# Cross attention of a perceiver layer: text probabilities and image sums travel with the image probabilities through DRAM, in halves, and a tile's queries are made between text and image scores

## The reference, cut to what matters

```python
HEADS = 16; DIM_HEAD = 64; INNER = 1024; TEXT_LEN = 77; IMG_SCALE = 1.0
def _attend(q, k, v):
    sim = jnp.einsum('bihd,bjhd->bhij', q, k) * SCALE
    attn = jax.nn.softmax(sim, axis=-1)
    out = jnp.einsum('bhij,bjhd->bihd', attn, v)
...
# Wq, Wk, Wv (text), Wk_ip, Wv_ip (image), Wo, bo
# x + (attend(q, k_text, v_text) + attend(q, k_image, v_image)) Wo + bo
```

## Time and profile before

| | |
|---|---|
| median of 3 runs | 2460.3 us (2457.01 to 2460.98) |
| the profiled execution | 2435.73 us |
| its span | 2433.6 us |
| TensorE matmul busy | 2160.2 us (89%) |
| VectorE busy | 1570.4 us (65%) |
| ScalarE busy | 925.0 us (38%) |
| GpSimd busy | 877.5 us (36%) |
| probabilities stored, loaded | 512 and 512 DMAs of 192 KB |

### The profile page before, as it was taken

One profiled execution on the slowest core, in us unless ns is written; L12 is line 12 of the kernel. 1 busy time (PEld: TensorE's weight loads), 2 busy tenths in 40 slices (PEclk: granted clock), 3 DMA queues, 4 the chain that ended last, 5 costly groups with the idle time before them and its releaser, 6 DMA issues. The chain is left out here.

```text
span 2433.6 us, 37422 instructions
## 1 busy us (share of the span) xinstructions
PE 2160.2 (89%) x13637; PEld 1726.1 (71%) x13637; DVE 1570.4 (65%) x2756; ACT 925.0 (38%) x1869; POOL 877.5 (36%) x535
## 2 busy tenths in 40 slices
PE   5878877796699999999999999999999997787897
PEld 3445545464598889888898998998998994334684
DVE  4179934333577677677677677777776763795554
ACT  1166611210244344344344444444443443452331
POOL 1066412431343333243343333343333300362455
PEclk8989977798899999999999999999999998798898
DMA  5800002511476677677676777776776656001364
GB/s 159 169 16 14 8 1 88 230 50 57 145 200 184 185 218 205 185 217 206 185 217 180 226 202 208 198 207 199 202 211 186 194 156 248 4 0 44 98 148 114
DMA packets 229957, 362.99 MB, mean 149 GB/s; under 512 B 41920, under 2 KB 197824, under 8 KB 225168
## 3 DMA queue, kind: packets, MB, share of 16 engines
q1 hardware_dynamic: 223008, 342.08, 48.1%
q0 software_dynamic: 6768, 18.49, 3.2%
HBM read 234.97 MB, written 125.50 MB: 148 GB/s over the span
## 5 line engine op out<-in xcount | busy, mean ns | idle before, releaser
L2271 PE MATMUL img_ps<-cn,pt_hi 128*128 128x256 f32 (+1 forms) x3072 | 569.7, 287 | 3.0 <-DVE pt_lo L2478 3.0
L2271 PEld LDWEIGHTS img_ps<-cn,pt_hi 128*128 128x128 f32 (+1 forms) x3072 | 477.3, 191 | 3.2 <-issue 3.2
L2271 PE MATMUL img_ps<-cn,pt_lo 128*128 128x256 f32 (+1 forms) x1536 | 435.9, 284 | 0.0
L2466 DVE STREAM_TRANSPOSE prob_blocks<-prob 128x384 f32<-128x384 f32 x512 | 250.6, 547 | 183.8 <-ACT prob L2402 175.9
L2248 PE MATMUL s_ps<-ct,a_hi 128*128 128x508 f32 x768 | 315.7, 411 | 0.0
L2249 PE MATMUL s_ps<-ct,a_hi 128*128 128x508 f32 x768 | 304.2, 396 | 0.0
L2250 PE MATMUL s_ps<-ct,a_lo 128*128 128x508 f32 x768 | 304.0, 396 | 0.0
L2001 POOL TENSOR_SCALAR ct<-staged 128x762 fp32r<-128x762 f32 x64 | 136.8, 2138 | 439.6 <-DMA staged<-in_ctx_t 312.5
L2271 PEld LDWEIGHTS img_ps<-cn,pt_lo 128*128 128x128 f32 (+1 forms) x1536 | 292.6, 190 | 0.0
L2478 DVE TENSOR_TENSOR pt_lo<-prob_moved,pt_hi 128x768 fp32r<-128x768 f32 x256 | 277.9, 1124 | 9.4 <-ACT pt_hi L2414 9.2
L2001 POOL TENSOR_SCALAR cn<-staged 128x768 fp32r<-128x768 f32 x64 | 137.4, 2147 | 376.5 <-DMA staged<-in_ctx_n 293.4
(11 more groups left out here) (370 smaller groups left out, 3712.9 us busy)
## 6 DMA issues: line engine op xcount, KB each, us to landing
prob_rows<-prob_blocks SPq DMA_DIRECT2D x512, 192.0 KB, 2.1
prob_moved<-prob_rows SPq DMA_DIRECT2D x512, 192.0 KB, 3.6
staged<-in_ctx_n SPq DMA_DIRECT2D x64, 384.0 KB, 4.7
staged<-in_ctx_t SPq DMA_DIRECT2D x64, 381.0 KB, 4.7
up_all_m<-in_up SPq DMA_DIRECT2D x8, 2048.0 KB, 12.8
down_all_m<-in_down SPq DMA_DIRECT2D x8, 1024.0 KB, 23.4
sums_m<-y_b SPq DMA_DIRECT2D x63, 128.0 KB, 2.2
w_shared<-in_wq SPq DMA_DIRECT2D x7, 1024.0 KB, 7.3
```

The source lines that it names most:

```text
L2271: last = nc.tensor.matmul(img_ps[:, 0:D], left[0:n, j, :], rows[0:n, right, j, :], start=j == 0 and at == 0, stop=j == IB - 1 and at == 2)
L2466: nc.vector.transpose(blocks[:, m], source[:, m]).then_inc(turned, 1)
```

## The change

The probabilities' DRAM round trip carries a bundle of 15 blocks of 128 columns instead of 12: the 12 image blocks of step g, one block with the scaled text probabilities of step g-3 and two with the scaled image sums of step g-3. So the three TensorE transposes and their copies are gone, and `value_side` reads its operands from `moved`, one iteration later than the transposes of that bundle (LAG = 3, loops to N + LAG + 2). The bundle is turned and stored in two halves instead of four quarters; it is loaded in four parts as before, 240 KB each. The text exponentials get buffers of their own.

`sums` multiplies `pt_hi` with both parts of `cn` in one matmul of 512 columns, into both halves of the bank, and `pt_lo` with the high part into the second half. ScalarE scales the second half into `prob`, VectorE scales the first half and adds it there. At a boundary the queries are made between text and image scores, and their copies come first on ScalarE and VectorE. The projection moves to iteration 4 of a tile, ahead of the sums. The bias is loaded within the stage into `head_out` and added on POOL before batch 1 is split. Text keys are loaded per batch (77 columns), Wq and Wo in two halves.

```diff
@@ load_stage @@
-            sp.dma_start(k.bo1[:], src["bo1"]).then_inc(rest_in, 16)
-            sp.wait_ge(rest_in, 48)
+            sp.wait_ge(rest_in, 32)
@@ cross_attention, sizes and buffers @@
-    RUN = IB * QR
+    TXT_AT, O_AT = IB, IB + 1
+    BUNDLE = IB + 1 + C
+    RUN = BUNDLE * QR
+    LAG = 3
+    PARTS = 2
+    PQ = Q // PARTS
...
-        prob = sb("prob1", [P, TXT + IB * P])
-        blocks = sb("prob_blocks", [P, Q, IB, QR])
-        block_rows = nc.dram_tensor("prob_rows", (2, Q, P, RUN), F32).ap()
-        moved = [sb(f"prob_moved{s}", [P, Q, IB, QR]) for s in range(2)]
+        prob = sb("prob1", [P, BUNDLE * P])
+        txt_prob = [sb(f"txt_prob{s}", [P, TXT]) for s in range(3)]
+        blocks = sb("prob_blocks", [P, Q, BUNDLE, QR])
+        block_rows = nc.dram_tensor("prob_rows", (2, PARTS, P, PQ, RUN), F32).ap()
+        moved = [sb(f"prob_moved{s}", [P, Q, BUNDLE, QR]) for s in range(2)]
         pt_hi, pt_lo = sb("pt_hi", [P, IB, P], F32R), sb("pt_lo", [P, IB, P], F32R)
-        pt_txt = [sb(f"pt_txt{s}", [P, P]) for s in range(3)]
...
+        bo = head_out[:, 0:C, :].rearrange("p c n -> p (c n)")
@@ SP @@
+                cols = slice(b % 2 * TXT, (b % 2 + 1) * TXT)
+                sp.dma_start(k_txt[:, heads], k.k_txt[b // 2][:, heads, cols]).then_inc(k_in, 16)
...
+            sp.dma_start(bo, src["bo1"]).then_inc(bo_in, 16)
...
-            for g in range(N):
+            for g in range(N + LAG):
                 s, (i, b, p, n) = g % 2, parts(g)
                 if g >= 2:
                     sp.wait_ge(moved_in[s], 16 * Q * (g // 2))
+                for u in range(PARTS):
+                    sp.wait_ge(turned, PARTS * g + u + 1)
+                    sp.dma_start(block_rows[s, u].rearrange("p m f -> p (m f)"),
+                                 blocks[:, quarters(u)].rearrange("p m j r -> p (m j r)")).then_inc(stored[u], 16)
+                if g >= 2:
+                    sp.wait_ge(split_done, 2 * min(g - 1, N))
+                if g > LAG + 1:
+                    sp.wait_ge(valued, g - LAG - 1)
                 for m in range(Q):
-                    sp.wait_ge(turned, Q * g + m + 1)
-                    sp.dma_start(block_rows[s, m], blocks[:, m].rearrange("p j r -> p (j r)")).then_inc(stored[m], 16)
-                if g >= 2:
-                    sp.wait_ge(split_done, 2 * (g - 1))
-                for m in range(Q):
-                    sp.wait_ge(stored[m], 16 * (g + 1))
+                    if m % PQ == 0:
+                        sp.wait_ge(stored[m // PQ], 16 * (g + 1))
                     sp.dma_start(moved[s][m * QR:(m + 1) * QR].rearrange("c a j r -> c a (j r)"),
-                                 block_rows[s, m].rearrange("(a c) f -> c a f", a=Q)).then_inc(moved_in[s], 16)
+                                 block_rows[s, m // PQ, :, m % PQ].rearrange("(a c) f -> c a f", a=Q)).then_inc(moved_in[s], 16)
+                if g >= N:
+                    continue
                 if g // PAIRS1 + 1 < NB:
                     load(g // PAIRS1 + 1, g % PAIRS1)
-                if n == 0 and i:
+                if p == 0 and g:
                     sp.wait_ge(scored, g)
-                    load_keys(i, 1)
+                    load_keys(g // PAIRS1, 1)
+                if p == 4 and g // PAIRS1 + 1 < NB:
+                    sp.wait_ge(scored, g)
+                    load_keys(g // PAIRS1 + 1, 0)
+                if n in (5, 6) and 1 <= i < NT - 1:
+                    sp.wait_ge(projected, i)
+                    sp.dma_start(wq[:, n - 5], src["wq1"][:, n - 5]).then_inc(wq_in, 16)
+                if n == 6 and i:
+                    sp.wait_ge(valued, i * STEPS)
+                    load_values(i, 1)
+                if n == 13 and i < NT - 1:
+                    sp.wait_ge(valued, i * STEPS + PAIRS1)
+                    load_values(i + 1, 0)
+                if n < 2 and i:
+                    heads = slice(n * PAIRS1 // 2, (n + 1) * PAIRS1 // 2)
                     sp.wait_ge(queried, i + 1)
-                    sp.dma_start(wo, src["wo1"]).then_inc(wo_in, 16)
-                if n == 4 and i:
-                    sp.wait_ge(v_used, 2 * i)
-                    load_values(i, 1)
-                if n == 5 and 1 <= i < NT - 1:
-                    sp.wait_ge(projected, i)
-                    sp.dma_start(wq, src["wq1"]).then_inc(wq_in, 16)
-                if n == 12 and i < NT - 1:
-                    sp.wait_ge(scored, i * STEPS + 12)
-                    load_keys(i + 1, 0)
-                if n == 13 and i < NT - 1:
-                    sp.wait_ge(v_used, 2 * i + 1)
-                    load_values(i + 1, 0)
+                    sp.dma_start(wo[:, heads], src["wo1"][:, heads]).then_inc(wo_in, 16)
@@ GpSimd @@
             split(0, range(4, 8))
+            pool.wait_ge(bo_in, 16)
+            nc.gpsimd.tensor_tensor(k.x[:], k.x[:], bo.unsqueeze(1).broadcast_to([P, NT, D]),
+                                    ALU.add).then_inc(bo_added, 1)
             split(1)
-            nc.gpsimd.tensor_tensor(k.x[:], k.x[:], k.bo1[:].unsqueeze(1).broadcast_to([P, NT, D]),
-                                    ALU.add).then_inc(bo_added, 1)
@@ TensorE @@
-            def turn_text(g):
-
-                bank = use()
-                pe.wait_ge(txt_normed, g + 1)
-                nc.tensor.transpose(t_ps[bank][0:TXT, 0:P], prob[:, 0:TXT], k.ident).then_inc(t_done[bank], 1)
...
-                        for at, (left, right) in enumerate(((pt_hi, 0), (pt_hi, 1), (pt_lo, 0))):
-                            last = nc.tensor.matmul(img_ps[:, 0:D], left[0:n, j, :], rows[0:n, right, j, :],
-                                                    start=j == 0 and at == 0, stop=j == IB - 1 and at == 2)
+                        nc.tensor.matmul(img_ps[:], pt_hi[0:n, j, :], rows[0:n, :, j, :], start=j == 0, stop=False)
+                        last = nc.tensor.matmul(img_ps[:, D:2 * D], pt_lo[0:n, j, :], rows[0:n, 0, j, :],
+                                                start=False, stop=j == IB - 1)
...
+                back = moved[(g + LAG) % 2]
+                pe.wait_ge(moved_in[(g + LAG) % 2], 16 * Q * ((g + LAG) // 2 + 1))
                 heads = [(t_ps[bank][r * S:(r + 1) * S, 0:S], slice((2 * p + r) * HD1, (2 * p + r + 1) * HD1),
-                          slice(r * S, (r + 1) * S)) for r in range(2)]
+                          slice(2 * r, 2 * r + 2)) for r in range(2)]
                 for c in range(C):
                     for out, cols, rows in heads:
-                        nc.tensor.matmul(out, wv[:, c, cols], ot[:, c, rows], start=c == 0, stop=False)
+                        nc.tensor.matmul(out, wv[:, c, cols], back[:, rows, O_AT + c, :], start=c == 0, stop=False)
                 for out, cols, rows in heads:
-                    last = nc.tensor.matmul(out, v_txt[0:TXT, b, cols], pt_txt[g % 3][0:TXT, rows],
+                    last = nc.tensor.matmul(out, v_txt[0:TXT, b, cols], back[0:TXT, rows, TXT_AT, :],
...
-            for g in range(N + 3):
+            for g in range(N + LAG + 2):
                 if g < N:
                     if g:
                         pe.wait_ge(exp_done, g)
                     kept(a_place)
                     text_scores(g)
+                    if boundary(g):
+                        if g > STEPS:
+                            pe.wait_ge(wq_in, 32 * (g // STEPS) + 16)
+                        q_places = queries(g // STEPS + 1)
                     scores(g)
-                if 1 <= g <= N:
-                    turn_text(g - 1)
-                if g >= 3:
-                    ot_place = turn_sums(g - 3)
-                if boundary(g):
-                    if g > STEPS:
-                        pe.wait_ge(wq_in, 16 * (g // STEPS) + 16)
-                    q_places = queries(g // STEPS + 1)
-                elif g < N - 1:
+                if g < N - 1:
+                    if boundary(g):
+                        for place in q_places:
+                            kept(place)
                     a_place = key_side(g + 1)
+                if projects(g) is not None:
+                    project(projects(g), head_place)
                 if 2 <= g <= N + 1:
                     sums(g - 2)
-                if boundary(g):
-                    for place in q_places:
-                        kept(place)
-                    a_place = key_side(g + 1)
-                if g >= 3:
-                    if g == 3:
+                if LAG + 1 <= g <= N + LAG:
+                    if g == LAG + 1:
                         pe.wait_ge(wv_in, 16)
-                    kept(ot_place)
-                    value_side(g - 3)
-                if projects(g) is not None:
-                    project(projects(g))
+                    value_side(g - LAG - 1)
+                    head_place = ring.place(1)
@@ ScalarE @@
+                if 2 <= g <= N + 1:
+                    act.wait_ge(summed, g - 1)
+                    act.wait_ge(inv_done, g - 1)
```

(29 more changed lines are left out.)

125 lines of the change are left out of this document (44 added, 81 removed).

## The result

The changed kernel took 2498.7 us, median of 4 runs (2491.9 to 2508.6), beside 2460.6 for the kernel before (4 runs, 2457.0 to 2463.5): ratio 1.016, 95% interval 1.013 to 1.019. A second set of runs (E1) gave 1.017 (1.014 to 1.021). The forecast was 2400, range 2374 to 2442.

A forecast was written before the change was run, and what follows sets the result against it. TensorE's own instructions were taken to bound the step. Gains 63 + 20 + 4 + 5 = 92 less 31.5 lost net 60.5 us: 2435.7 profiled becomes 2375, carried over to the runs' median as 2400, range 2374 to 2442.

The forecast's parts named there:

- The return: Bundle's DRAM round trip before the value side: landing S+13.6 to 13.7 (S: start of its first reduction); 15 us lost.
- The loop of two steps: From a bundle's reductions through its value side: with landing L, step is the larger of 9.62 and (L + 5.15)/2.
- the ride: Text probabilities and sums carried in the bundle, replacing three TensorE transposes per step; the transposes' removal was priced at 42 us.
- Tail: Stage's end: last sums pass transposes, store and loads before the value side; 8.5 us plus 1 for lower clock, 9.5 lost.
- The unheld step: Plain cross attention step on TensorE: 0.50 us shorter, 9.62 instead of 10.12; 63 us over 128 steps.
- The transposes: Text transpose and two transposes of the sums removed from TensorE: 0.33 us a step, 42 us over 128 steps.
- Boundaries: Queries of a new tile placed before the image scores, removing waits and low clock: 20 us gained, bounds 13 and 23.
- The bias: Output bias addition on POOL moved from step 8 to the stage's start: 5 us gained, 2 lost at the start.
- the 512 column term: Sums on TensorE in 12 matmuls of 512 and 12 of 256 columns: 0.16 us a step, 21 us saved.
- The term of 5 us for VectorE: VectorE's last operation in contested steps ends at S+9.66 against 9.62, late by under 0.1 us: 5 us lost in all.
- the slower rival: Return landing past S+15.4 makes steps 10.26 and eats all other gains; at S+16, step 10.58 and 2499 us; chance 0.11.
- The sign named beforehand: Forecast wrong if the value side waits in every step; it expected waits for the return in some steps only.

The follow-up runs named there:

- E1: The changed kernel run again without alteration, beside the kernel before on the same chip: 2487.5 us, ratio 1.017.
- E10: Changed kernel, loads leaving out three of the 15 blocks from the third step on, stores unchanged: 2408.7 us, 0.982 of the kernel before.
- E11: Changed kernel with no context loaded from batch 2 on: 2483.7 us, 1.013 of the kernel before.
- E7: Changed kernel with each context piece cut to 48 KB from batch 2 on: 2462.7 us, 1.004 of the kernel before.
- E3: Changed kernel with the bundle turned and stored in four quarters instead of two halves: 2431.0 us, 0.994 of the kernel before.
- E2: Changed kernel with value side and projection one iteration later, same data and buffers: 2407.4 us, 0.985 of the kernel before.
- E4: Kernel before with sums in 512 columns, queries early and bias early, text and sums not put in the bundle: 2409.5 us, 0.986.
- E5: Kernel before with only a tile's queries moved between text and image scores: 2429.7 us, 0.990.
- E9: E8 with the last three bundles turning, storing and loading only their three live blocks: 2381.5 us, 0.971 of the kernel before.
- E6: Kernel before with only the sums changed, to 12 matmuls of 512 columns and 12 of 256: 2447.1 us, 0.997.
- E8: Changed kernel with both the value side one iteration later and quarters instead of halves: 2390.2 us, 0.976 of the kernel before.
- E12: Changed kernel with the context piece issued only when the step's loads have landed, ahead of the next stores: 2657.8 us, 1.084.

## Why the prediction was wrong

**The step that failed is "The return".** It put the last landing at S+13.6 to 13.7, against a need of S+14.1, and let a third of the steps be 0.7 us late: 15 us. Measured is S+15.7 in the median and past S+14.1 in all 111 steps. The value side waited in 66 of them, 1.2 us on average: 80.6 us. The landing is 2.1 us later than forecast, and three terms of it were mis-sized (figures of single loads are medians by order of issue, from the trace's records):

- The last load got the median of all loads, 3.6 us. But the value side waits for the last of four, and that one took 4.2 us already in the kernel before. That is 0.6 us, and it stood in the trace of before.
- The extra of the loads was counted about once (48 KB, 0.2 us). The four loads of a step run together and fill the engines at 216 GB/s, so the last carries the extra of all four, 0.9 us: it takes 5.4 us where 4.2 and 0.2 would be 4.4. I had written this down as the upper bound, 14.5, and the earlier trace rows said it: 0.96 busy means that no load has room to grow in. E10 shows it.
- The stores: 2.9 us forecast, 3.6 measured. The 2.9 is right when the context is out of the way (2.8 in E10, with less to load, and in E11, 2.9 in E7). A later store shifts all loads behind it: the last one goes out at S+10.2 for S+9.8, 0.4 us. E3 shows what the halves cost at the front of this chain: 56 us.

The loop of two steps, on the other hand, held. Where the value side had waited, it started 0.13 us after the landing, and the next step but one began 5.16 us later, for the 5.15 of the forecast. With L = 15.7 the formula gives 10.4 us a step. Measured are 1229.9 us over 111 steps; less 13 sets of 32 matmuls for queries and projections (3.66 each) and 26 for the half clock they are 10.4 a step. That only 66 of the steps show a wait doesn't mean that the others were in time: a step lengthened by a wait gives the bundle behind it the room. The step ahead of a value side without a wait took 12.6 us in the median, ahead of one with a wait 9.8.

The gains of E2, E3 and E10 (80, 56 and 85 us) don't add up; each removes the same lateness of one to two microseconds once.

The Trainium skill's page "DMA: Bandwidth & Descriptors" (Anatomy of one DMA) fits 2.0 us plus bytes at 436 GB/s to DMAs issued by GpSimd. As an estimate for the DMAs of SP here that gives 2.6 us for a load of 240 KB and 3.1 for a store of 480. Measured are 4.5, and 2.8 to 3.6. The fit describes one DMA; the four loads of a step here are one queue of work, and the measurement decides. Nor do these figures give the 0.5 us of margin that the prediction takes from them: with 3.1 for the store and 2.6 for the load in place of its 2.9 and 3.8 it would be 1.0 us.

**The clock.** That a wait for the return costs more than its length was in the sum only for the projection at the end. In the 111 steps the half clock took 51 us in 14 stretches, 14 us in 3 before: at half speed some (51 - 14)/2 = 19 us. The three before stand behind waits at boundaries and are gone in E4 and E5, so they are already in the gain of the boundaries; beside E4 the ride's half clock costs 26 us.

**Tail.** 9.5 us forecast, 18.5 measured. I followed one bundle through its return; two are waited for in full behind the last scores, the one for 6.11 us and the next for 7.40, and the projection ran at the low clock (2.5 us) where I took 1. E9 shows that 8.5 us of it are the twelve empty blocks.

**What was right.** The unheld step: 9.66 (E2: 9.69 median) for 9.62. The transposes: 0.33 us a step forecast, 0.35 measured (E4's plain step of 10.04 less 9.69). The two transposes of a bundle on VectorE: 2.2 and 2.24 (line L2474). Boundaries: 20 us and 23 measured (E5); a boundary behind a step without a wait now takes 9.7 + 3.6:

```profile
1330.61 0.45 PE L2300 MATMUL t_ps<-prob_moved,wv 128*64 128x64 f32 x8
...
1331.39 3.78 PE L2237 MATMUL t_ps<-h_t,w_shared 128*128 128x128 f32 x32
...
1343.85 0.45 PE L2300 MATMUL t_ps<-prob_moved,wv 128*64 128x64 f32 x8
```

From L2300 to L2300 it is 13.24 us. The projection's wait of 0.55 is gone. The bias: 5 forecast at steps 8 and 9, 5.5 measured (E4). Too large was the 512 column term: 21 us forecast, 7 measured, for the reason told at E6.

**The sum by the runs.** The three parts without the ride bring 36 us where I had 44 (21 + 20 + 3). The ride was forecast to gain 42 + 4 - 15 - 5 - 9.5 = 16.5 and cost 78. The traces of E1 and E4 show where. In the 111 steps E1 is 59 us longer: the wait 79 more, the half clock 27 more (54.6 us of it, none in E4), the transposes 0.35 x 111 = 39 less, and waits of E4 that are gone 7.5 less, together 60. The first 16 steps, which have late returns too, are 8 us longer and the end 17. That is 84, and the two profiled executions differ by 83. The term of 5 us for VectorE has no row of its own: L2300's is the only wait of TensorE in the changed kernel's window.

**The rivals.** What happened is the mechanism of the slower rival (0.11): the landing past S+15.4 in the median step. Its price of 2499 meets the median of 2498.7 partly by luck. It is for a landing at S+16 and leaves out the half clock and the longer end; with the measured S+15.7 the loop's step is 10.4 and not 10.58, and the clock and the end make up for it. Single steps lie between 9.66 and over 12. I held against this rival that ScalarE had waited only 1.2 us for the loads. That showed that the old deadline was far off, and nothing about the new one. The sign named beforehand, a wait of the value side in every step, was too strict: the wait showed in 66 of 111 steps, though the landing was late in all.

## What to carry over

When a consumer is moved behind a round trip, compare its deadline with the landing of the step's last transfer, the late ones included, not with a median over all transfers, and give it a whole step of room if a buffer allows it: here one iteration more was worth 80 us, with an end of 47.0 us against 47.4 (E2, E1). When several DMAs of one step fill the engines together, bytes added to each are paid by the last one for all of them. And a transfer at the front of a chain should stay in small parts, even at the price of more instructions (E3, E8).

## What the runs showed of the hardware

- With four loads to 32 partitions each under way, the 16 DMA engines moved 212 to 216 GB/s at a busy share of 0.96 to 1.10. The stage in E9 runs at 0.91 busy and 250 GB/s with TensorE at 0.99, so DMA engines as busy as that were no bound there, where nothing stood at its deadline.
- The last of a step's four loads took 4.2 us where the median of all four was 3.6 (192 KB each), and 5.4 where it was 4.5 (240 KB each).
- A context piece beside the loads left them at 4.4 to 4.5 us, whether whole, small or absent; issued right ahead of the stores it took their landing from 3.6 to 4.9 us, and the kernel's time rose by 6.7% (1.084 over 1.016) (E12).
- The granted clock fell to half in 14 stretches of about 3.6 us in the changed kernel's steps, each of them at a wait of 1.6 us or longer; 14 other waits of 1.5 us or more drew none, and no shorter wait did. There were 44 stretches of about 4.2 us in E12, whose waits go up to 4.1 us, and none in the steps of E10, whose 35 waits are 1.5 us at most. Which of the longer waits bring it down I can't tell from these.
- The first block of sums after another kind of matmul is 0.08 us slower than the rest, in either shape. A pitch taken over a group with its first member in it is too high.
